# Two-layer transformer on one core: the first layer's expert outputs are stored one row per token and choice, and TensorE adds the four

## The reference, cut to what matters

```python
_, idx = jax.lax.top_k(scores + bias[None, :], K)        # K = 4 of E = 32
w = w / jnp.clip(jnp.sum(w, axis=-1, keepdims=True), 1e-12, None)
pos = position of this (token, choice) among those of its expert
valid = pos < C                                          # C = 128
xe = zeros((E, C, D)).at[eid, posc].add(where(valid, Xrep, 0))
h = silu(xe @ W1) * (xe @ W3)
ye = h @ W2
yrows = ye[eid, posc] * gflat[:, None]                   # gflat: w, 0 where not valid
out = yrows.reshape(-1, K, D).sum(axis=1)                # the four choices of a token
out = out + silu(X @ sw1.T) * (X @ sw3.T) @ sw2.T
```

## Time and profile before

| | us |
|---|---|
| median of the runs | 2004.95 |
| profiled execution: its time | 2002.02 |
| profiled execution: span of the core | 2000.1 |
| route phase, in the trace | 504.7 to 684 |
| experts phase | 684 to 800 |
| project phase | 800 to 1012 |

### The profile page before, as it was taken

One profiled execution on the slowest core, in us unless ns is written; L12 is line 12 of the kernel. 1 busy time (PEld: TensorE's weight loads), 2 busy tenths in 40 slices (PEclk: granted clock), 3 DMA queues, 4 the chain that ended last, 5 costly groups with the idle time before them and its releaser, 6 DMA issues. The chain is left out here.

```text
span 2000.1 us, 50931 instructions
## 1 busy us (share of the span) xinstructions
PE 1612.7 (81%) x17727; PEld 1252.1 (63%) x17727; DVE 1473.4 (74%) x4099; ACT 1185.8 (59%) x2762; POOL 1096.3 (55%) x1141
## 2 busy tenths in 40 slices
PE   5599999998788695698847777777789607999994
PEld 4478888887577442344325555555568607999993
DVE  8688888887499542699979999999667624555556
ACT  4566666665279721577828888887366404565551
POOL 3278888887000286233348888888437773444440
PEclk8799999999899798799969999999766658999998
DMA  4000000000501132521000000000401112222216
GB/s 120 18 3 3 4 4 4 4 3 3 219 28 41 42 45 35 147 63 43 11 0 1 1 2 1 1 1 1 185 23 48 52 60 62 66 64 65 64 51 257
DMA packets 84954, 92.34 MB, mean 46 GB/s; under 512 B 11696, under 2 KB 69296, under 8 KB 84000
## 3 DMA queue, kind: packets, MB, share of 16 engines
q1 hardware_dynamic: 67840, 62.66, 9.9%
q0 software_dynamic: 14560, 22.24, 4.3%
q10 hardware_dynamic: 2304, 4.20, 0.5%
HBM read 46.14 MB, written 42.91 MB: 45 GB/s over the span
## 5 line engine op out<-in xcount | busy, mean ns | idle before, releaser
L2275 POOL TENSOR_TENSOR delta_A<-delta_A,delta_sW 128x256 f32<-128x256 f32 x256 | 193.7, 757 | 79.1 <-ACT delta_sW L2122 53.0
L2045 PE MATMUL delta_u<-delta_m,tables_sb 128*128 128x256 f32 x512 | 166.7, 407 | 82.0 <-DVE delta_m L2195 82.0
L694 ACT ACTIVATE attn_p_att<-attn_score,attn_mx 128x32 f32<-128x32 f32 (+7 forms) x512 | 150.4, 409 | 134.7 <-DVE attn_mx L756 134.7
L2895 POOL DMA_INDIRECT choice_rows<-ffn_y,ffn_xg x135 | 129.7, 961 | 170.9 <-DVE ffn_y L3002 167.4
L2122 ACT ACTIVATE delta_sW<-delta_W,tables_sb 128x256 f32<-128x256 f32 x256 | 126.7, 506 | 79.9 <-DVE delta_W L2217 76.1
L2045 PEld LDWEIGHTS delta_u<-delta_m,tables_sb 128*128 128x128 f32 x512 | 87.1, 190 | 132.7 <-DVE delta_m L2195 126.0
L2041 PE MATMUL delta_u<-delta_v_own,tables_sb 128*128 128x256 f32 x512 | 153.8, 383 | 8.7 <-DVE xnT L2182 8.7
L2852 POOL DMA_INDIRECT rows<-mix_rows,mix_slot x128 | 125.5, 980 | 47.9 <-issue 38.6
L1324 POOL DMA_INDIRECT exp_rows<-rows,slot_token x32 | 33.1, 1033 | 190.4 <-SPq L142 180.9
L2217 DVE TENSOR_TENSOR delta_W<-delta_W,delta_u 128x128 f32<-128x128 f32 x512 | 133.1, 280 | 4.5
L2204 DVE TENSOR_TENSOR delta_u<-delta_u,delta_prod 128x256 f32<-128x256 f32 x256 | 109.8, 429 | 17.8 <-PE delta_u L2045 4.2
(11 more groups left out here) (396 smaller groups left out, 4691.4 us busy)
## 6 DMA issues: line engine op xcount, KB each, us to landing
ffn_xg<-rows SPq DMA_DIRECT2D x135, 66.0 KB, 1.8
acc<-route_zero SPq DMA_DIRECT2D x10, 832.0 KB
comb_rows<-choice_rows SPq DMA_DIRECT2D x32, 256.0 KB, 5.3
rows<-route_rows SPq DMA_DIRECT2D x8, 640.0 KB, 3.5
load_rows<-in_x SPq DMA_DIRECT2D x16, 256.0 KB, 3.8
bT<-acc SPq DMA_DIRECT2D x16, 256.0 KB, 4.1
qT<-acc SPq DMA_DIRECT2D x16, 256.0 KB, 4.7
x_kept<-xT SPq DMA_DIRECT2D x16, 256.0 KB, 2.1
```

Of the source, the lines that this page charges most:

```text
L694: last = nc.scalar.activation(p_att[:, gr, PAIR_OFF[n]:PAIR_OFF[n] + SLOT * (n + 1)], S[:, gr, c:c + SLOT * (n + 1)], ACT.Exp, bias=mx[:, ...
L2045: nc.tensor.matmul(corrections(h, pp % 2), g.t("same_head"), m1[:, h].rearrange("p t d b -> p (t d b)"), start=False, stop=True).then_inc( ...
L2275: nc.gpsimd.tensor_tensor(A[:, t % 8], A[:, (t - 1) % 8], sW[:, t % RING], ALU.add).then_inc(k.A, 1)
L2895: nc.gpsimd.indirect_dma_start(g.choice_rows, bass.IndirectOffsetOnAxis(xg[:, n % RING, D:D + 1].bitcast(U32), 0), y[:, n % RING, :], None ...
```

## The change

Route writes two DRAM indices per slot instead of one. The third weighed copy of the one-hot rows now holds the number `tile * 4 + choice`; it is made by one POOL instruction per `i` (L1319 in the new file) instead of eight small ones of ACT. At the end DVE splits the number into tile and choice (12 instructions where there were 5) and makes `slot_token` and `slot_choice`. Free slots of expert e point to a row of their own behind the last token's. The array in DRAM is `by_choice`, 8192 x 4 rows, so 16.8 MB are zeroed in place of 8.5 MB. In the experts phase the indirect DMA stores rows and does not add, and waits for none of the earlier ones. In the project phase SP loads four rows per token (two DMAs of 512 KB per half in place of two of 256 KB), POOL's addition is gone, and `turn` is four multiplications by the identity per tile that add up in PSUM, 32 per round, in place of one transposition, 8 per round. Half 1 of a pair lands in `vT` and in a new tile `spare_rows`.

```diff
@@ route, SP
-            for n in range(2):
-                acc = g.acc[n].rearrange("(p r) c -> p (r c)", p=128)
-                for i in range(5):
-                    sp.dma_start(acc[:, i * 13 * D:(i + 1) * 13 * D], zero[:, :]).then_inc(c.zero_out, 16)
+            choices = g.by_choice[0:N * K0, :].rearrange("(p r) c -> p (r c)", p=128)
+            for i in range(ZEROS):                       # 16
+                sp.dma_start(choices[:, i * 16 * D:(i + 1) * 16 * D], zero[:, :]).then_inc(c.zero_out, 16)
@@ route, PE add_slots
                 pe.wait_ge(c.spread, i + 1)
+                pe.wait_ge(c.numbered, i + 1)
@@ route, ACT weigh
-                nc.scalar.activation(by_expert[:, at, 1], by_expert[:, at, 0], ACT.Copy, scale=g.t("row_no")[:, 0:1])
-                for j in range(SIDE):
-                    last = nc.scalar.activation(by_expert[:, at, 2, j * K0:(j + 1) * K0], by_expert[:, at, 0, j * K0:(j + 1) * K0],
-                                                ACT.Copy, scale=float(i * SIDE + j))
-                last.then_inc(c.spread, 1)
+                nc.scalar.activation(by_expert[:, at, 1], by_expert[:, at, 0], ACT.Copy, scale=g.t("row_no")[:, 0:1])\
+                    .then_inc(c.spread, 1)
@@ route, POOL (new)
+            for i in range(0, LAST + 1):
+                pool.wait_ge(c.route, STEPS * i + MASKED - 2)
+                if i > 1:
+                    pool.wait_ge(c.slots_added, i - 1)
+                nc.gpsimd.tensor_tensor(by_expert[:, i % 2, 2], by_expert[:, i % 2, 0],
+                                        number[:, i * CHOICES:(i + 1) * CHOICES][:, :, None].to_broadcast([128, CHOICES, E0]),
+                                        ALU.mult).then_inc(c.numbered, 1)
@@ experts, POOL
-                added = (c.added0, c.added1)[e % 2]
-                if e > 1:
-                    pool.wait_ge(added, 16 * (e // 2))
-                nc.gpsimd.indirect_dma_start(g.acc[e % 2], bass.IndirectOffsetOnAxis(g.slot_token[:, e:e + 1], 0),
-                                             y[:, e * D:(e + 1) * D], None, compute_op=ALU.add).then_inc(added, 16)
+                nc.gpsimd.indirect_dma_start(g.by_choice, bass.IndirectOffsetOnAxis(g.slot_choice[:, e:e + 1], 0),
+                                             y[:, e * D:(e + 1) * D], None).then_inc(c.sent, 16)
@@ project, SP rows_of
-                        sp.wait_ge(k[par].summed, i - 1)
+                        sp.wait_ge(k[par].turned, i - 1)
+                    first = (i * PAR + par) * CH * K0
+                    rows = g.by_choice[bass.ds(first, CH * K0), :].rearrange("(r p n) c -> p r n c", p=128, n=K0)
                     for n in range(2):
-                        sp.dma_start(row_parts(i, par)[n], g.acc[n][cols(i, par), :].rearrange("(r p) c -> p r c", p=128))\
+                        sp.dma_start(row_parts(i, par)[n], rows[:, :, n * (K0 // 2):(n + 1) * (K0 // 2), :])\
@@ project, PE turn
-                    pe.wait_ge(k[par].summed, i + 1)
+                    pe.wait_ge((k[par].rows_even, k[par].rows_odd)[i % 2], 32 * (i // 2 + 1))
                     for r in range(TILES):
-                        last = nc.tensor.transpose(front[par][:, 128 * r:128 * r + 128], row_parts(i, par)[0][:, r, :], g.t("ident"))
+                        for n in range(K0):
+                            last = nc.tensor.matmul(front[par][:, 128 * r:128 * r + 128],
+                                                    row_parts(i, par)[n // (K0 // 2)][:, r, n % (K0 // 2), :], g.t("ident"),
+                                                    start=n == 0, stop=n == K0 - 1)
@@ project, POOL
-                    nc.gpsimd.tensor_tensor(one, one, other, ALU.add).then_inc(k[par].summed, 1)
```

More of the change, by code:

```diff
@@ L957, in route_phase @@
         ones = s.sb("ones", [128, 128], BF16)
-        zero = s.sb("zero", [128, 13 * D])
+        zero = s.sb("zero", [128, 16 * D])
         zero_bf = s.sb("zero_bf", [128, 128], BF16)
@@ L981, in route_phase @@
         own = s.sb("own", [128, SIDE, K0, E0])
+        number = s.sb("number", [128, NCH // PAR * CHOICES], BF16)
+        whole = s.sb("whole", [128, E0], mybir.dt.int32)
+        tile_of = s.sb("tile_of", [128, E0])
         slot = s.sb("slot", [128, CHOICES])
@@ L992, in route_phase @@
                    " logits turned score rows_read route mask placed counted owned slot spread off by_slot slots_added"
-                   " slots_done held tail by_slot_rest")
+                   " slots_done held tail by_slot_rest numbers numbered")
         rows_out = [s.sems("rows_out", n).rows_out for n in range(2)]
@@ L1283, in _ @@
             dve.wait_ge(c.held, 1)
+            nc.vector.tensor_copy(whole[:, :], held[:, 2, :]).then_inc(c.tail, 1)
             nc.vector.tensor_scalar(free[:, :], held[:, 0, :], -1.0, 1.0, ALU.mult, ALU.add).then_inc(c.tail, 1)
-            nc.vector.scalar_tensor_tensor(held[:, 1, :], held[:, 2, :], 128.0, held[:, 1, :], ALU.mult, ALU.add)\
-                .then_inc(c.tail, 1)
             dve.wait_ge(c.tail, 2)
+            nc.vector.tensor_scalar(whole[:, :], whole[:, :], 2, None, ALU.arith_shift_right).then_inc(c.tail, 1)
@@ L1288, in _ @@
             nc.vector.scalar_tensor_tensor(held[:, 1, :], free[:, :], g.t("past"), held[:, 1, :], ALU.mult, ALU.add)\
                 .then_inc(c.tail, 1)
-            dve.wait_ge(c.tail, 3)
-            nc.vector.tensor_copy(g.slot_token[:, :], held[:, 1, :])
+            dve.wait_ge(c.tail, 4)
+            nc.vector.tensor_copy(tile_of[:, :], whole[:, :]).then_inc(c.tail, 1)
+            dve.wait_ge(c.tail, 5)
+            nc.vector.scalar_tensor_tensor(held[:, 1, :], tile_of[:, :], 128.0, held[:, 1, :], ALU.mult, ALU.add)\
+                .then_inc(c.tail, 1)
@@ new lines, in _ @@
+            nc.vector.scalar_tensor_tensor(held[:, 2, :], tile_of[:, :], -float(K0), held[:, 2, :], ALU.mult, ALU.add)\
+                .then_inc(c.tail, 1)
+            dve.wait_ge(c.tail, 7)
+            nc.vector.tensor_copy(g.slot_token[:, :], held[:, 1, :])
+            nc.vector.scalar_tensor_tensor(held[:, 2, :], held[:, 1, :], float(K0), held[:, 2, :], ALU.mult, ALU.add)\
+                .then_inc(c.tail, 1)
+            nc.vector.tensor_tensor(free[:, :], free[:, :], g.t("iota")[:, 0:E0], ALU.mult).then_inc(c.tail, 1)
@@ new lines, in _ @@
+            dve.wait_ge(c.tail, 9)
+            nc.vector.scalar_tensor_tensor(held[:, 2, :], free[:, :], float(K0 * CAP), held[:, 2, :], ALU.mult, ALU.add)\
+                .then_inc(c.tail, 1)
+            dve.wait_ge(c.tail, 10)
+            nc.vector.tensor_copy(g.slot_choice[:, :], held[:, 2, :])
+        @block.gpsimd
+        def _(pool):
+            for n in range(2):
+                nc.gpsimd.tensor_scalar(number[:, n * 128:(n + 1) * 128], g.t("iota")[:, 0:128], 128.0 * n, None, ALU.add)\
+                    .then_inc(c.numbers, 1)
+            pool.wait_ge(c.numbers, 2)
+            for i in range(0, LAST + 1):
[5 more added lines that the diff above has]
+                                        ALU.mult).then_inc(c.numbered, 1)
@@ L1527, in row_parts @@
         def row_parts(i, par):
-            return [x[:, cols(i, par)].rearrange("p (r c) -> p r c", c=D) for x in (g.bT, g.qT)]
+            pair = bass.ds(i * (PAR * CH), PAR * CH)
+            first, second = (g.vT[:, pair], spare_rows[:, i % 2, :]) if par else (g.bT[:, pair], g.qT[:, pair])
+            return [x.rearrange("p (r n c) -> p r n c", n=K0 // 2, c=D) for x in (first, second)]
         def unit(i, par):
@@ L1891, in _ @@
         def _(pool):
-            def sum_rows(i):
-                for par in both:
-                    pool.wait_ge((k[par].rows_even, k[par].rows_odd)[i % 2], 32 * (i // 2 + 1))
-                    one, other = row_parts(i, par)
-                    nc.gpsimd.tensor_tensor(one, one, other, ALU.add).then_inc(k[par].summed, 1)
             def fix(i):
@@ L3175, in build @@
         g.slot_token = ctx.enter_context(nc.sbuf_tensor("slot_token", [128, E0], U32))
+        g.slot_choice = ctx.enter_context(nc.sbuf_tensor("slot_choice", [128, E0], U32))
         g.rows = nc.dram_tensor("rows", (N + CAP, ROW), F32, kind="Internal").ap()
[L3177 removed]
+        g.by_choice = nc.dram_tensor("by_choice", ((N + E0 * CAP) * K0, D), F32, kind="Internal").ap()
         g.x_kept = nc.dram_tensor("x_kept", (128, N), F32, kind="Internal").ap()
```

15 lines of the change are left out of this document (6 added, 9 removed).

## The result

The changed kernel takes 2031.14 us (median of 5 runs, 2029.24 to 2033.75), the kernel before 2003.12 us (5 runs, 2000.40 to 2006.43): 1.014 times as long, 95% interval 1.0126 to 1.0154. It is slower. The range 2018 to 2055 holds the time; the forecast of 2038 is 7 us too high. In the profiled executions 2002.02 us stand against 2031.94.

The account below looks back on a forecast made before the run. Project was taken as bound by DVE with PE near, experts by POOL, route by busy PE, DVE and ACT. Terms -12.0 + 39.5 + 5.1 + 1.9 = +34.5 on 2002.0 gave 2036.5; forecast 2038 us, range 2018 to 2055.

Parts of the forecast that it names:

- Experts, -12.0: Experts phase: plain stores of 0.96 us, PE's 5.28 us rounds (-9.8), quicker landing (-2.2); bounds -14 and -8.
- the landing: End of experts: the wait from last store's end to next phase's first DMA falls from 8.2 to 6.0 us, -2.2.
- Project, +39.5: Project phase: first two turns +11, six later turns +31.3, POOL's addition gone -2.8; bounds +29 and +51.
- the two first turns: Start of project, partly at the low clock: +6 us for the first turn and +5 for the second.
- rival C: Project start stays at low clock or first rows late, first turns cost 22 us; or POOL takes 3: 2047 or 2054; chance 0.14.
- Rival B: Project turns hidden in DVE's other work, if 64 instructions take below about 2.1 us: 1996 us; chance 0.06.
- Route, +7.0: Route phase: DVE's mask held by POOL's multiplication, +5.1 us, and the longer tail, +1.9.
- The tail: End of route: twelve small DVE instructions in place of five before the first gather, +1.9 us; bounds 1.2 and 2.6.
- Rival A: Route phase: DVE isn't held by POOL's multiplication, -7 + 1.9 us in place of +7.0: 2024 us; chance 0.18.
- The zeros and the double reading, free: Route: 8.3 MB more zeros cost nothing, some 6 us spare; project: 2 MB per round in place of 1, free.
- The total: Whole kernel: 2002.0 + 34.5 = 2036.5 us, 2039.5 against the median; 2038 was said, between them.

Follow-up runs that it names:

- e2: The kernel before, with the experts' stores writing over the rows and not adding (sum over a token's choices left out): 1991.39 us, 0.9941.
- e1: The changed kernel, with TensorE turning only the first of a token's four rows, all rows still read: 1989.07 us, 0.9933 of the kernel before.
- e4: The changed kernel, with weighed rows kept in bf16 and summed in fp32, half the zeros, stores and reads: 1988.66 us, 0.9936 of the kernel before.
- e9: The changed kernel, with the project phase's turn ahead of the second widen step in TensorE's order: 2045.02 us, 1.0216 of the kernel before.
- e3: The changed kernel, with POOL's route multiplication started two steps later, after VectorE's masks: 2026.22 us, 1.0122 of the kernel before.
- e10: The changed kernel, with POOL's route multiplication started when the inverse roots are made: 2028.10 us, 1.0137 of the kernel before.
- e5: The changed kernel, with a second buffer of 16.8 MB zeroed beside the first in the route phase: 2063.09 us, 1.0312 of the kernel before.
- e6: The changed kernel, with POOL adding a token's four rows and TensorE turning one row by transposition: 2037.72 us, 1.0179 of the kernel before.
- e14: The changed kernel with weighed rows as two bf16 rows, the second made behind the next round's hidden product, and the edits of e10 and e7: 1995.19 us.
- e7: The changed kernel, with 16 identity products ahead of the project phase's first turn and 24 behind the first back: 2034.78 us, one run.

## Why the prediction was right, point by point

- *Experts, -12.0: measured -11.9*, by parts a little differently. The pace came as said: stores of 0.97 us, PE's 5.28 us, POOL no more the bound; e2 showed that the adding alone was the price. But the landing gave 0.6 us (8.2 to 7.6) and not 2.2: the 6.0 us of the earlier trace rows were read at another phase's entry, and e2, with plain stores in the kernel before, has 7.7 us here. From the first output to the last store's end it was 11.6 us rather than 9.8: 91.6 before (700.18 to 791.76), 80.0 after. The last round has no next shared product in it and is 3.2 us long, which 15 rounds of 5.28 left out. Two errors of opposite sign, 1.6 and 1.8 us, made the sum right: that it came within 0.1 us is luck. (The first output came 0.3 us later behind the phase's start.)
- *Project, +39.5: measured +38.7.* DVE waits 2.49 and 2.70 us (2.4 and 2.7 said), L1831 is at 0.30, rounds are 27.54 us (27.5 said). The first q product starts 35.4 us behind the phase's start for 25.1: +10.3 for the two first turns, 11 said. The clock rose 3.6 us into the first turn, which took 9.0 us and the second 8.4, so rival C with its 13.6 didn't come. e1 and e4 took the instructions away by number and by time, and the phase gave all of it back; e9 is against the rival in which the turn's place is at fault. Rival B was wrong by its own bound: 64 instructions take 7.1 us and not 2.1.
- The Trainium skill's rule on transposition and the clock gate ("TensorE: Matmul & The Clock Gate", Part 4: PE-mode transpose) fits what came: after 3.6 us of multiplications the level was 2.4 GHz, in the earlier trace rows not in 7 us of little but transpositions. No run here puts the same load on PE in both forms, so the rule is not shown, only not contradicted.
- *Route, +7.0: measured +6.4.* POOL's instruction takes 2.14 us (2.1 said), the mask 1.87 for 0.29: held 1.58 (1.75 said), of which 0.86 a round is left (0.99 said), the rest went into the wait of the earlier trace rows, now gone. The five rounds cost 4.0 us (5.0 said), the last two 1.0 (0.1 said). The tail is 2.33 us for 1.07: +1.3, 1.9 said. Here too the sum is nearer than its parts. Rival A fell: e3 moved POOL's instruction only, and the hold moved with it; e10 moved it again, and little of it was left.
- *The zeros and the double reading, free:* right at this size (e4 and e5 for the zeros, e1 for the reading). The spare time was said to be 6 us and is about 9. What the prediction didn't say, and e5 does at its one size, is what comes behind that: 33.5 us of the whole core for 39 us more of zeros.
- *The total*, 2036.5 worked out against the profiled 2002.0, is 2031.9: of the 4.6 us too much, 4.9 are the mix phase's clock, which no term of the sum could hold; the other phases' errors nearly cancel. Another 1.5 came from going halfway to the median.

How the hold works was cited from the Trainium skill, "GPSIMD Engine Reference", 8. Key points: contention for DVE instructions in a two-port mode or with two SBUF inputs. The trace agrees for instructions with two SBUF inputs: the mask, 1.87 us for 0.29, those of e6, and the product in e10. The tensor_scalar instructions that were held (1.30 us for 0.17 in e3, 0.98 for 0.30 in e6) have one SBUF input; no run here shows which mode they run in. What the runs add is that the later one waits and the earlier isn't interrupted.

## What to carry to other kernels

Before moving work to another engine, look at who waits for whom in a steady round: here a saving of 12 us on an engine that was the bound by 1.1 us a round was paid with 39 us on one that stood directly in front of the bound. If a sum is moved to TensorE, price it in instructions: fp32 counts twice and each is twice as long (0.111 us for 0.056), so bf16 turns the same idea into a gain (e4), and two bf16 parts, with two further edits, into a small one (e14). Put GpSimd's two-operand work beside VectorE instructions that read PSUM or reduce: those passed beside it here, and a tensor_scalar on one SBUF operand did not. And look at how far a free transfer is from its landing's first reader.

## What the runs showed of the hardware that I had not expected

- An indirect DMA that adds costs POOL 1.60 us to issue and a plain one 0.97, while from the last store's end to the next phase's first DMA it takes only 0.6 us more (8.2 for 7.6).
- POOL's fp32 additions hold DVE's fp32 instructions of two SBUF operands up to POOL's end (0.43 to 2.47 us), and in e6 PE's granted clock fell to 1.2 GHz behind the 3.9 us in which PE then stood: 6.5 us a round were lost against the 22.9 of before.
- The routed rows' DMA, issued behind the bulk zeros while the DMA engines were full (share 1.01, 427 GB/s), kept a whole core waiting for 33.9 us in e5.
- The moment at which the clock rises in a phase differs between profiles in which that phase's code is the same: the mix phase took 229.86 us in the kernel after and 234.58 in e7.
